# The border between the expert stage and layer 1, reordered on three engines

## The reference, cut to what matters

```
x = L0_attn_x
xn = _layernorm(x, axis=-1)
s = _L0_attn_ref(xn, ...)            # a linear recurrence along the sequence
g = _silu(_L0_ffn_ref(xn, ...))      # 4 of 32 experts by row, and a shared expert
x = x + s * g
xn = _layernorm(x, axis=-1)
s = _L1_attn_ref(xn, wq, bq, wk, bk, wv, bv)    # softmax attention in each sequence
g = _silu(_L1_ffn_ref(xn, ...))                 # 2 of 8 experts by row, gates from a softmax of the two best
x = x + s * g
```

## Time and profile before

| | us |
|---|---|
| median of 3 runs | 456.23 (455.85 to 458.99) |
| the profiled execution's own time | 457.9 |
| its span, first to last instruction | 456.0 |
| VectorE busy in the span | 319.6 (70%) |
| TensorE busy in the span | 381.0 (84%) |
| GpSimd busy in the span | 275.7 (60%) |

### The profile page before, as it was taken

How to read it: one execution, slowest core, us unless ns; L and a number is a source line. 1 busy time by engine, 2 the same in 40 slices (tenths; PEclk the granted TensorE clock), 3 DMA queues, 4 the chain that set the end, 5 groups by cost and what they waited for, 6 DMA issues and landing times. The chain is left out here.

```text
span 456.0 us, 8825 instructions
## 1 busy us (share of the span) xinstructions
PE 381.0 (84%) x2582; PEld 349.4 (77%) x2582; DVE 319.6 (70%) x1153; ACT 257.6 (56%) x505; POOL 275.7 (60%) x324
## 2 busy tenths in 40 slices
PE   0596986995089999997999897967998998889994
PEld 0584875884089999996999797856987977779983
DVE  6869588769137667766567648682699999995643
ACT  2233124421046767764776564537898886788882
POOL 5935777777777777763777777527777877100000
PEclk9999798898579999999999998978999999899998
DMA  7899995111257667537677563412222222000000
GB/s 183 257 376 310 291 390 180 53 54 46 90 176 213 215 224 219 201 127 240 196 227 217 171 207 101 139 54 56 64 60 70 67 58 65 24 14 25 12 24 23
DMA packets 45902, 65.16 MB, mean 143 GB/s; under 512 B 8586, under 2 KB 23331, under 8 KB 45859
## 3 DMA queue, kind: packets, MB, share of 16 engines
q1 hardware_dynamic: 37666, 47.83, 33.0%
q0 software_dynamic: 8192, 16.79, 12.6%
HBM read 28.93 MB, written 35.65 MB: 142 GB/s over the span
## 5 line engine op out<-in xcount | busy, mean ns | idle before, releaser
L550 POOL DMA_INDIRECT slot_rows<-xn_tok,slot_of x128 | 126.8, 991 | 49.7 <-issue 38.7
L564 POOL DMA_INDIRECT onehot<-expert_rows,slot_of x64 | 64.9, 1014 | 38.3 <-DMA expert_rows<-zeros 19.4
L564 POOL DMA_INDIRECT route_tmp<-expert_rows,slot_of x64 | 63.0, 985 | 19.5 <-issue 19.5
L1399 DVE TENSOR_TENSOR act<-sg,ps 128x384 f32<-128x384 f32 x48 | 26.5, 553 | 49.5 <-ACT sg L1007 48.6
L738 PE MATMUL ps<-w_dn,actT 96*128 x384 | 53.1, 283 | 5.1 <-ACT zeros L1016 5.1
L738 PEld LDWEIGHTS ps<-w_dn,actT 96*128 96x128 f32 x384 | 48.1, 197 | 5.9 <-issue 5.9
L1007 ACT ACTIVATE sg<-ps 128x384 f32<-128x384 f32 x48 | 23.5, 489 | 37.9 <-PE ps L747 37.2
L722 PE MATMUL ps<-ident,rows 128*128 128x128 f32 x192 | 29.9, 280 | 13.2 <-DMA rows<-slot_rows 11.6
L747 PE MATMUL ps<-w_gu,raw_fc 128*128 x192 | 37.8, 342 | 1.2 <-DVE act L1399 0.5
L1016 ACT COPY zeros<-ps 128x512 f32<-128x512 f32 x48 | 28.1, 585 | 17.7 <-PE ps L738 17.6
L824 PE MATMUL ps<-prT,rows 128*128 128x128 f32 x256 | 34.4, 291 | 3.4 <-DVE raw_fc L1548 3.4
(11 more groups left out here) (240 smaller groups left out, 899.1 us busy)
## 6 DMA issues: line engine op xcount, KB each, us to landing
slot_rows<-zeros SPq DMA_DIRECT2D x12, 1024.0 KB, 12.0
rows<-slot_rows SPq DMA_DIRECT2D x48, 256.0 KB
expert_rows<-zeros SPq DMA_DIRECT2D x48, 256.0 KB
x_tok<-in_L_attn_x_dram SPq DMA_DIRECT2D x8, 256.0 KB, 5.5
slot_rows<-xn_tok,slot_of POOLq DMA_INDIRECT x128, 2.4
out_dram<-raw_fc SPq DMA_DIRECT2D x16, 128.0 KB, 1.8
w_dn<-in_L_ffn_w_down_dram SPq DMA_DIRECT2D x1, 1536.0 KB, 17.1
onehot<-expert_rows,slot_of POOLq DMA_INDIRECT x64
```

Of the source, the lines that this page charges most:

```text
L550: g.indirect_dma_start(out=slot_rows[r], out_offset=bass.IndirectOffsetOnAxis(ap=slot_of[:, n:n + 1], axis=0), in_=xn_tok[:, r * HT + t, : ...
L564: g.indirect_dma_start(out=gath[b % 4][:, j, :], out_offset=None, in_=expert_rows[r], in_offset=bass.IndirectOffsetOnAxis(ap=slot_of[:, n: ...
L1399: v.tensor_tensor(act[u][:].rearrange("p (a b) i -> p a b i", a=2), sg[u][:].rearrange("p (a b) i -> p a b i", a=2), ps[:, 1 + 2 * u:3 + 2 ...
```

## The change

- **VectorE.** Behind hidden(47) now stand make_gates(0), sum_experts(7), mix(3), least(0), and only then stats1, rstd1 and norm1 of pair 3.
- **TensorE.** first_products, project(0) and values(0), stands in step 47 between act_T(47) and down(46). project(0) writes PSUM bank 1 in place of bank 6. down(47) writes bank 0, and doesn't wait for copy_out(46). scores(0) waits for copy_out(46) alone, hidden_of(0) for the last hidden, and the loop for copy_out(47).
- **ScalarE.** first_kept, shift_projected(0) and keep_values(0), stands in step 47 between copy_aT(47) and copy_out(46). silu_f(3) moves from the end of step 46 to the end of step 47, behind copy_out(47).

No instruction is added or taken away.

```diff
+        def down_bank(n):
+            return 0 if n == N - 1 else 6
...
                 pe.wait_ge(e_aTs, n + 1)
-                if not first:
+                if not first and n < N - 1:
                     pe.wait_ge(e_out, n)
...
+            def first_products():
+                pe.wait_ge(biases, 2)
+                pe.wait_ge(c_lgs, FSEQ // 2 - 1)
+                pe.wait_ge(e_act, N - 1)
+                project(0)
+                values(0)
...
+                if n == N - 1:
+                    turn = first_products
...
-            pe.wait_ge(e_out, N)
-            pe.wait_ge(c_lgs, FSEQ // 2 - 1)
...
-            project(0)
-            values(0)
+            pe.wait_ge(e_out, N - 1)
             scores(0)
+            pe.wait_ge(e_act, N)
+            hidden_of(0)
+            pe.wait_ge(e_out, N)
...
+            def first_kept():
+                sc.wait_ge(biases, 2)
+                shift_projected(0)
+                keep_values(0, 0)
...
-                if step == 2:
+                if (step == 2 and n < N - 2) or n == N - 1:
                     after = lambda: silu_f(q)
...
+                if n == N - 1:
+                    turn = first_kept
...
-            shift_projected(0)
-            keep_values(0, 0)
...
-                if step == 3:
+                if step == 3 and n < N - 1:
                     mix(q, False)
                     stats1(q)
...
-                if step == 2 and n == N - 2:
-                    sum_experts(2 * q + 1)
-            rstd1()
-            norm1(FSEQ // 2 - 1)
...
             make_gates(0)
+            sum_experts(FSEQ - 1)
+            mix(FSEQ // 2 - 1, False)
             least(0, 0)
+            stats1(FSEQ // 2 - 1)
+            rstd1()
+            norm1(FSEQ // 2 - 1)
```

More of the change, by code:

```diff
@@ L734, in down @@
                 pe.wait_ge(e_aTs, n + 1)
-                if not first:
+                if not first and n < N - 1:
                     pe.wait_ge(e_out, n)
                 for j in range(GT):
-                    mm = pe.matmul(ps[:, 6, j * P:(j + 1) * P], actT[u][:, j * P:(j + 1) * P],
+                    mm = pe.matmul(ps[:, down_bank(n), j * P:(j + 1) * P], actT[u][:, j * P:(j + 1) * P],
                                    w_dn[:, bass.ds(e[j] * P, P)], start=True, stop=True)
@@ L797, in stage_e, with turned_rows, project, values @@
                     down(n, n % 2, ids(n * GT))
+            def turned_rows(b):
+                return xn_tok[:, b * 2:b * 2 + 2, :]
+            def project(b):
+                pe.wait_ge(c_xn_kept, b // 2 + 1)
+                if b:
+                    pe.wait_ge(d_nmx, b)
+                pe.matmul(ps[:, 6 if b else 1, 0:SEQ], w1T[:, 0:P], turned_rows(b), start=True, stop=True).then_inc(d_qk, 1)
+            def values(b):
+                if b:
+                    pe.wait_ge(d_vs, b)
+                for j in range(2):
+                    pe.matmul(ps[:, 7, j * VW:(j + 1) * VW], ones_bf[:], bv_rows[:], start=True, stop=False)
+                    mm = pe.matmul(ps[:, 7, j * VW:(j + 1) * VW], turned_rows(b)[:, j, :], w1T[:, P:P + VW],
+                                   start=False, stop=True)
+                mm.then_inc(d_v, 1)
             for n in range(N):
@@ L840, in _ @@
             pe.wait_ge(biases, 2)
[L842 to L860, removed]
             def scores(b):
@@ L900, in output @@
                 mm.then_inc(d_o, 1)
-            project(0)
-            values(0)
+            pe.wait_ge(e_out, N - 1)
             scores(0)
+            pe.wait_ge(e_act, N)
+            hidden_of(0)
+            pe.wait_ge(e_out, N)
             for b in range(NSEQ):
                 u = b % 2
-                hidden_of(b)
+                if b:
+                    hidden_of(b)
                 if b:
@@ L1015, in copy_out @@
                     sc.wait_ge(e_stored[slot], rnd * 16)
-                a.copy(eo[slot], bank(6)).then_inc(e_out, 1)
+                a.copy(eo[slot], bank(down_bank(n))).then_inc(e_out, 1)
             for r in range(NH):
@@ L1065, in stage_e, with shift_projected, keep_values @@
                     after()
+            def shift_projected(b):
+                sc.wait_ge(d_qk, b + 1)
+                if b:
+                    sc.wait_ge(d_s, b)
+                a.activation(key_of, ps[:, 6 if b else 1, 0:SEQ], ACT.Identity, bias=w1T[:, 2 * P + 1:2 * P + 2],
+                             scale=-SCALE).then_inc(d_qks, 1)
+            def keep_values(b, u):
+                sc.wait_ge(d_v, b + 1)
+                if b >= 2:
+                    sc.wait_ge(d_o, b - 1)
+                a.copy(v_sb[u], ps[:, 7, 0:2 * VW].rearrange("p (a d) -> p a d", a=2)).then_inc(d_vs, 1)
+            def first_kept():
+                sc.wait_ge(biases, 2)
+                shift_projected(0)
+                keep_values(0, 0)
             def tanh_gates(k):
@@ L1085, in _ @@
                     after = lambda: tanh_gates(0)
+                if n == N - 1:
+                    turn = first_kept
+                    sc.wait_ge(sent[1], 16 * HT * TOP0)
                 if half_starts(n):
@@ L1088, in _ @@
                 stage_e(n, turn, after)
-            sc.wait_ge(sent[1], 16 * HT * TOP0)
             def tanh_f(p):
```

## The result

| | kernel before | changed kernel |
|---|---|---|
| median, us | 458.11 (455.13 to 461.60, 11 runs) | 454.20 (452.02 to 455.86, 11 runs) |
| ratio | | 0.9913, interval 0.9887 to 0.9939 |
| the profiled execution, us | 457.9 | 452.02 |
| its span, us | 456.0 | 450.1 |

The changed kernel is faster by 0.87%, or 3.9 us. I had forecast 5.7 us and 450.6, with a range up to 453.0: the time lies above the range, and the gain is two thirds of the forecast one. The kernel before has moved too: the 456.23 from which I subtracted was the median of three runs, and with eight more it is 458.11. On that base the forecast would have read 452.4, inside the range.

A forecast was written before the change was run, and what follows sets the result against it. The border into layer 1, a chain changing engines, was taken as the bound, with VectorE's least the later chain. 6.66 earlier less 0.98 for gathers gives 5.68; from the 456.23 median, 450.6, range 449.0 to 453.0.

The forecast's parts named there:

- Gates: Border, VectorE: make_gates(0), 2.24 us, moves into the 2.43 us idle ahead of sequence 7's sum and costs nothing.
- first products: Border, TensorE: early project and values delay down(46) by 0.55; down(47) ends about 297.35 instead of 301.33, at upper level.
- norm behind least: Border, VectorE: least starts 6.66 us earlier; statistics and norm, 4.81, then cost nothing, with 1 us to spare before gate_hidden(0).
- ScalarE's price: Border, ScalarE: silu_f behind copy_out(47) makes mix and all that follows it 0.39 us later.
- The table for the exponentials (1.28): Border, ScalarE: the table loads from 298.5 to 299.8, before least ends at 300.86.
- Rival 4: Layer 1, TensorE: lower clock after idle stretches; slower from 5.7 us of such work, 460.6 at 10 us; chance 0.03.
- came back at once: Argument against rival 4: before, the clock stood at 0.50 in the border and recovered when layer 1's work ran.
- One of my own signs of being wrong: Sequence 0, TensorE: a long stretch at 0.50 would show the prediction wrong.
- The gathers: Sequences 8 to 15: start 4.02 earlier, readers 6.66; sequence 15's sum waits 1.80, of which 0.98 is left as loss.
- the prediction's 0.2 us: Gathers' pace: if VectorE contention slows them, the slow part begins two gathers sooner, losing 0.2 us: 450.8 for 450.6.
- The landing of 2.96: Sequence 15: from its last gather's start to its rows being there, the middle of 2.48 and 3.44.
- the forecast's sum of 5.68: Whole kernel: least's 6.66 us earlier start, less 0.98 lost to the gathers, gives 5.68 us less.

The follow-up runs named there:

- The two halves alone: Kernel before with only VectorE's new order: 458.07, ratio 0.9993; changed kernel with VectorE's old order, keeping TensorE's and ScalarE's half: 459.09, ratio 1.0027.
- Kept busy: Changed kernel plus six filling matmuls on TensorE between turn_shares(0) and spread_gates(0), written to a PSUM bank nobody reads: 454.51, ratio 0.9916.
- one wait less: Changed kernel without ScalarE's second wait for the biases, ahead of layer 1's loop: 453.64, ratio 0.9903.
- both edits: Changed kernel without ScalarE's second wait for the biases and with six filling matmuls on TensorE in sequence 0: 452.33, ratio 0.9851.
- the kernel with fewer gathers: Changed kernel without ScalarE's second biases wait, with six filling matmuls, and 6 instead of 8 gathers for each of sequences 8 to 15: 449.27, ratio 0.9785.
- the second set: Changed kernel unaltered, timed again on the chip of the last two experiments: 453.77, ratio 0.9881.

## Why the prediction was right or wrong

*Gates, first products, norm behind least: right.* Least came 6.74 earlier for 6.66. The norm ended at 305.46 + 1.21 = 306.67, 2.23 us ahead of gate_hidden(0), so it cost nothing. ScalarE's price was 0.64 for 0.39. The two halves alone show that neither does it without the other: VectorE's waits 6.83 us for scores, and the other half ends later than before.

*"The table for the exponentials (1.28) is loaded from 298.5 to 299.8, before least ends": this step failed.* I saw that there was time for the load, and took it that a load waits for nothing, since it didn't before. I hadn't asked which instruction carries which wait. The load stood behind least and cost 1.28 to 1.34 us at the entrance, and 2.14 by gate_hidden(1), with the clock that follows; taking the needless wait away gave exactly that back, and with it the forecast's instant of the exponentials (6.73 earlier). It did not give back the time: 453.64 for 454.20, ratio 0.9903 for 0.9913. So this is the step of the mechanism that failed, but it is not shown to be what put the time outside the range. The Trainium skill, "ScalarE: Activation LUTs", section "Step-by-step: what each stage is for", says that the compiler places the load right before the instruction that needs it. The listing agrees; that a wait of this instruction may stand ahead of the load, the listing and the trace showed here.

*Rival 4's mechanism came true in small.* TensorE's idle stretch ahead of spread_gates(0) grew from 2.41 to 2.94, and sequence 0 took 10.62 us for 9.78 before: 0.84 lost. My sum had no term for it. Against it I held that the clock "came back at once" in the kernel before, and that was read too short: it did come back for project(1), but it fell again from 312, as the windows above show. One of my own signs of being wrong, a long stretch at 0.50 in sequence 0, came true. Kept busy, TensorE stays at the upper level and sequence 0 takes 8.58. This was never near the 5.7 us from which it would have decided.

*The gathers: the mechanism was right, but not yet in force in this kernel.* I had 0.98 us for them. In the changed kernel they cost nothing: the table and the clock had held layer 1 back, and the last gather of the half came 4.65 earlier, 0.76 more than the first. So the gathers did not become slower by the prediction's 0.2 us: from the first gather to the last it was 82.5 us for 83.3 before, and 82.2 to 82.6 in the six other traces with all gathers. That is scatter larger than the term, so it decides nothing about the cause of the slower pace. The landing of 2.96 was sized well: 2.94 from the last gather to the sum that waited for it with one wait less, 2.61 with both edits. With one wait less the waits came at sequence 12 first (0.61), which the prediction didn't name, and at 15 (0.30). They cost about 0.7 to 1.0, near the 0.98. With both edits the waits are 3.23.

*Why the mends are worth so little* is therefore shown only in part. With one wait less 2.14 at gate_hidden(1) leaves 0.40 at the last one, and with TensorE kept busy 2.46 leaves 0.02. Waits for gathers took 0.7 to 1.0 in the first case and 0.7 in the second. TensorE's lower clock took 0.4 to 0.7 between gate_hidden(8) and (9) in the first, and 0.9 and 0.7 in two stretches of the second. With both edits the waits for gathers are the main cause, as the kernel with fewer gathers shows. The last gate_hidden comes 5.74 earlier than before with one wait less, near the forecast's sum of 5.68, and 5.34 or 4.93 earlier in the changed kernel. But the span ends 5.8 earlier with one wait less and 6.9 or 6.4 in the changed kernel, because the last sum met the lower clock in the one and not in the other. So the nearness to 5.68 is in part luck.

*Between gate_hidden(1) and the last gate_hidden* the changed kernel wins 0.78 back on the kernel before. 0.70 of it lies between gate_hidden(8) and (9): 7.96 us in both executions of the changed kernel, 8.66 before and in the kernels with one wait less or with TensorE kept busy. TensorE waits there about 2.7 us for least in the kernel before and in the changed one; in the changed one its project(9) already runs at the lower level (1.19 for 0.67), and its values(9) at the upper one again (0.22 for 0.32). So the clock fell and came back earlier there, and before, the lower level reached as far as the work that gate_hidden(9) waits for. What decides when it falls was not tried.

*The number.* The time of 454.2 lies 3.6 us above the forecast of 450.6, and two terms of the sum make that up. The larger is the base: 456.23 was the median of three runs, and the kernel before measured 458.11, 458.88 and 460.11 in larger sets, 1.9 us more in the one beside which the 454.2 was timed. The ratio 0.9913 on 456.23 would be 452.3, inside the range. The other is the gain: 3.9 us by the first medians against 5.7, and 5.5 us by the ratio of the second set (0.9881). The failed steps above don't account for these missing 1.8 us: counted from the last hidden, the traces of the changed kernel win 4.9 to 5.3 up to the last gate_hidden and 6.4 to 6.9 up to the end of the span. What they show besides is that the last hidden itself comes later, at 293.19 and 295.30 for 292.23 before. The start of the second half is shortest, 10.5 and 11.5 us, in the two traces with TensorE's and ScalarE's old programs, and 11.6 to 14.3 in the seven with the new ones. The instructions up to there are the same, and two against seven can't tell an effect of the change from chance; no run was made for it. So the cause of this part stays open.

## What to carry to other kernels

When work is moved past a wait, look where the wait itself ends up: one that was already paid for, left standing ahead of an instruction that brings a table load with it, pushed another wait ahead of the load and cost the load's whole time. And when a border is shortened, list what starts on clocks of its own there (here the gathers, which wait for stores): each part that the others win beyond its room comes back as a wait. Each new wait can also move a stretch in which TensorE's clock is low, and so a mend of 2.1 or 2.5 us was worth 0.4 or nothing here. When executions scatter by more than the effect, count instants from the last event that the change doesn't touch, but count them to the end of the span, and look at the granted clock before calling a difference the change's own.

## What the runs showed of the hardware

Six matmuls that nobody reads, 2.76 us of TensorE's time, held the granted clock at 1.00 through a stretch in which it stood at 0.50 to 0.69 without them, and sequence 0 took 8.58 us for 10.62. The clock did not fall alike behind equal idle stretches: with 1.20 us ahead of project(7) it fell in one kernel and not in another (the sum behind it took 3.07 and 2.02 us), and behind the same idle stretches at the end the last sum took 2.02 us in five traces and 3.42 to 3.62 in four. An ACT_TABLE_LOAD that stood behind least's wait added its 1.28 us to the path; ahead of the wait it was hidden. The start of the second half, from copy_out(23) to copy_out(24), took between 10.5 and 14.3 us in executions with the same instructions up to there. The last store's landing varied too: from the last hidden to the first gather it was 8.69 to 10.29 us in seven executions with the same order of copies.
